# The state products of a batch gathered ahead of its four read-outs in a chunked RWKV layer

## The reference

```python
def step(s, rkvw):                       # s: state of a head, 16 x 16
    r_t, k_t, v_t, w_t = rkvw
    a = k_t[:, :, :, None] * v_t[:, :, None, :]
    out = jnp.einsum('bhk,bhkd->bhd', r_t, u * a + s)
    return (a + w_t[:, :, :, None] * s, out)
xs = tuple((jnp.moveaxis(t, 1, 0) for t in (r, k, v, w)))
_, outs = jax.lax.scan(step, s0, xs)     # 128 steps; s0 comes with the input
att = jnp.moveaxis(outs, 0, 1).reshape(b, l, E)
```

## Time and profile before

| what | us |
|---|---|
| median of 3 runs | 1643.91 (1643.78 to 1644.02) |
| the profiled execution | 1644.96 |
| its span, first to last instruction | 1643.2 |
| PE busy | 1560.6 (95%) |
| PE weight loads busy | 1156.4 (70%) |
| DVE busy | 966.8 (59%) |
| POOL busy | 604.9 (37%) |
| ACT busy | 518.5 (32%) |
| a round in the steady part (`V0` of round 7 at 763.55, of round 8 at 860.77) | 97.22 |

### The profile page before, as it was taken

One profiled execution on the slowest core, in us unless ns is written; L12 is line 12 of the kernel. 1 busy time (PEld: TensorE's weight loads), 2 busy tenths in 40 slices (PEclk: granted clock), 3 DMA queues, 4 the chain that ended last, 5 costly groups with the idle time before them and its releaser, 6 DMA issues.

```text
span 1643.2 us, 45840 instructions
## 1 busy us (share of the span) xinstructions
PE 1560.6 (95%) x19880; PEld 1156.4 (70%) x19880; DVE 966.8 (59%) x1990; ACT 518.5 (32%) x910; POOL 604.9 (37%) x512
## 2 busy tenths in 40 slices
PE   7989799999999999999999999999999999999888
PEld 7767576777777677776767677677767767777554
DVE  2555647567574755757475674746657475664542
ACT  1213323234232333323233233333323223342331
POOL 2442414426152442615335261432525244251411
PEclk9989899999999999999999999999999999999998
DMA  7010101102020110202011020200102011010200
GB/s 278 6 46 11 52 21 42 42 21 64 6 64 23 35 50 12 72 6 63 24 34 51 5 66 20 61 25 24 62 4 65 22 35 50 8 64 7 70 11 26
DMA packets 56424, 67.72 MB, mean 41 GB/s; under 512 B 23264, under 2 KB 40032, under 8 KB 55200
## 3 DMA queue, kind: packets, MB, share of 16 engines
q1 hardware_dynamic: 56224, 64.79, 12.3%
HBM read 43.75 MB, written 8.39 MB: 32 GB/s over the span
## 4 chain that ended last, share of the span: by engine, by line
PE 79%; DVE 9%; ACT 5%; POOL 5%; issue 3%; DVEq 0%; ACTq 0%; POOLq 0%
PE pair L1132 35%; PE pair L1140 17%; PE at_ps L1066 3%; PE at_ps L1059 3%; PE pair L1164 2%; POOL x L472 2%; PE kv_ps L1088 2%; DVE bonv L576 2%; PE att_ps L1123 2%; PE pair L1185 2%; ACT at L889 2%; POOL cen L498 2%; DVE x L695 1%; PE pair L1221 1%; PE pair L1148 1%
## 5 line engine op out<-in xcount | busy, mean ns | idle before, releaser
L1132 PE MATMUL pair<-x,wts 128*128 128x256 f32 x2048 | 467.0, 384 | 12.7 <-POOL x L472 12.6
L1132 PEld LDWEIGHTS pair<-x,wts 128*128 128x128 f32 x2048 | 382.6, 190 | 74.6 <-DVE x L695 14.6
L472 POOL TENSOR_TENSOR x<-x,xnT 128x1024 f32<-128x1024 f32 x80 | 173.5, 2178 | 300.8 <-DVE x L695 300.8
L695 DVE SCALAR_TENSOR_TENSOR x<-pair,vecs,sx 128x256 f32<-128x256 f32 x320 | 131.1, 476 | 199.0 <-PE pair L1164 150.2
L889 ACT ACTIVATE at<-at_ps 128x512 f32<-128x512 f32 x128 | 76.2, 595 | 204.6 <-PE at_ps L1066 202.2
L576 DVE SCALAR_TENSOR_TENSOR bonv<-rT,vecs,kT 128x128 f32<-128x128 f32 x128 | 59.1, 522 | 126.8 <-ACT rT L880 116.8
L483 POOL TENSOR_TENSOR bonv<-bonv,p 128x256 f32<-128x256 f32 x32 | 40.2, 1258 | 215.4 <-DVE p L711 215.4
L1066 PE MATMUL at_ps<-rm,kc 128*16 128x128 f32 (+1 forms) x2048 | 111.0, 276 | 0.0
L1140 PE MATMUL pair<-wts,sx 128*128 128x512 f32 x240 | 107.0, 599 | 4.1 <-ACT cen L875 4.1
L1140 PE MATMUL pair<-wts,cen 128*128 128x512 f32 x240 | 110.8, 604 | 0.0
L1140 PE MATMUL pair<-wts,yT 128*128 128x512 f32 x240 | 107.2, 599 | 0.8 <-POOL yT L510 0.8
(11 more groups left out here) (194 smaller groups left out, 2616.9 us busy)
## 6 DMA issues: line engine op xcount, KB each, us to landing
rm<-rst SPq DMA_DIRECT2D x1024, 12.0 KB, 1.8
xu<-in_x SPq DMA_DIRECT2D x16, 512.0 KB, 4.1
wts<-in_wts SPq DMA_DIRECT2D x8, 1024.0 KB, 13.8
kvs<-in_s SPq DMA_DIRECT2D x32, 256.0 KB, 2.9
s<-in_s SPq DMA_DIRECT2D x32, 256.0 KB, 2.9
x<-in_x SPq DMA_DIRECT2D x15, 512.0 KB, 4.6
out<-sx SPq DMA_DIRECT2D x15, 512.0 KB, 3.0
prev<-in_prev SPq DMA_DIRECT2D x32, 4.0 KB, 3.9
```

Source lines behind the costliest of these rows:

```text
L472: gp.tensor_tensor(t, t, xnT[:, :, :, 1:L1].rearrange("p g b t -> p (g b) t"), ALU.add).then_inc(x5_ready, 1)
L695: last = ve.scalar_tensor_tensor(seqs(x5[q], g), ps[:, :, g * L:(g + 1) * L], vecs[:, vec, g:g + 1], seqs(sx, g), ALU.add, ALU.mult)
L1132: last = pe.matmul(ps[:, g // 2, TB * (g % 2):TB * (g % 2 + 1)], wts[:, m, k, g * P:(g + 1) * P], source[:, k, :], start=(k == 0), stop=(k ...
```

## The change

The products with the states leave `read_out` and become a task of their own, `st0` or `st1`: eight products in a row (four units, two states), behind the waits that stood in `V0` or `V4`. In PE's lists `st0` stands right ahead of `V0`, `st1` right ahead of `V4`. A `V` now is its wait for `E` and its sixteen small products. The new semaphore `states_read` counts the two tasks, and the loads of `s0` and `kvs` wait for it and no longer for `read_done`. `S0` then waits for the `st1` of the round before, where it waited for that round's `V7`; `S1` and `F0` wait for `st0`, where they waited for `V3`. The lists of all other engines are unchanged, SP's too.

```diff
-PE_ORDER = [... "A0", "wv.1", "V0", "c02_1", "c1v_1", "A1", "V1", ...
-            "V4", "wo.0", ...
+PE_ORDER = [... "A0", "wv.1", "st0", "V0", "c02_1", "c1v_1", "A1", "V1", ...
+            "st1", "V4", "wo.0", ...
...
             def load_s0(blk, b):
-                if blk.past(UNITS, G * b):
-                    sp.wait_ge(read_done, blk.count(UNITS, G * b))
+                if blk.past(2, b):
+                    sp.wait_ge(states_read, blk.count(2, b))
...
             def load_first(blk, b):
-                if blk.past(UNITS, 4 * (b + 1) - UNITS):
-                    sp.wait_ge(read_done, blk.count(UNITS, 4 * (b + 1) - UNITS))
+                if blk.past(2, b - 1):
+                    sp.wait_ge(states_read, blk.count(2, b - 1))
...
+            def from_states(at_, b):
+                pe.wait_ge(kvs_ready, at_.count(2, b + 1))
+                pe.wait_ge(s0_in, at_.count(32, 16 * (b + 1)))
+                pe.wait_ge(rchain, at_.count(2 * NR, NR * (b + 1)))
+                if at_.past(2, b - 1):
+                    pe.wait_ge(attT_ready, at_.count(2, b - 1))
+                for g in range(G):
+                    pe.matmul(att_ps[:, 0, b, g, :], s0[:, g, :], rst[:, b, g, R64A:RST], start=(g == 0), stop=False,
+                              skip_group_check=True)
+                    last = pe.matmul(att_ps[:, 1, b, g, :], kvs[b][:, g * P:(g + 1) * P], rst[:, b, g, R64B:R16C],
+                                     start=(g == 0), stop=False, skip_group_check=True)
+                last.then_inc(states_read, 1)
+
             def read_out(at_, n):
                 b, g = n // G, n % G
                 o = att_ps[:, :, b, g, :]
-                if g == 0:
...
-                pe.matmul(o[:, 0, :], s0[:, g, :], rst[:, b, g, R64A:RST], start=(g == 0), stop=False,
-                          skip_group_check=True)
-                pe.matmul(o[:, 1, :], kvs[b][:, g * P:(g + 1) * P], rst[:, b, g, R64B:R16C], start=(g == 0),
-                          stop=False, skip_group_check=True)
                 pe.wait_ge(at_ready, at_.count(UNITS, n + 1))
```

More of the change, by code:

```diff
@@ L61 @@
     "kt0": 0, "kt1": 0, "kv0": 0, "kv1": 0, "F0": 1, "F1": 0, "dec0": 0, "dec1": 0, "attb1": -1, "attb0": 0, "aT1": -1, "aT0": 0}
-PE_ORDER = ["mixWV", "kt0", "V7", "kv0", "wv.0", "aT1", "A0", "wv.1", "V0", "c02_1", "c1v_1", "A1", "V1", "z", "v.0",
+PE_ORDER = ["mixWV", "kt0", "V7", "kv0", "wv.0", "aT1", "A0", "wv.1", "st0", "V0", "c02_1", "c1v_1", "A1", "V1", "z", "v.0",
             "decay", "v.1", "A2", "V2", "mixKR", "A3", "V3", "yT", "k.0", "k.1", "mixG", "kt1", "A4", "kv1", "r.0", "aT0", "r.1",
-            "V4", "wo.0", "wo.1", "A5", "g.0", "g.1", "x2T", "V5", "xT", "c02_0", "A6", "V6",
+            "st1", "V4", "wo.0", "wo.1", "A5", "g.0", "g.1", "x2T", "V5", "xT", "c02_0", "A6", "V6",
             "kk.0", "kk.1", "c1v_0", "rr.0", "rr.1", "h", "A7"]
@@ L84 @@
                 "g.1", "h", "c1v_0"],
-           LAST: ["kt0", "V7", "kv0", "wv.0", "aT1", "A0", "wv.1", "V0", "A1", "c02_1", "V1", "c1v_1", "A2", "V2",
-                  "yT", "A3", "V3", "kt1", "wo.0", "kv1", "wo.1", "aT0", "A4", "V4", "yT@0", "A5", "V5", "x2T", "A6", "V6",
+           LAST: ["kt0", "V7", "kv0", "wv.0", "aT1", "A0", "wv.1", "st0", "V0", "A1", "c02_1", "V1", "c1v_1", "A2", "V2",
+                  "yT", "A3", "V3", "kt1", "wo.0", "kv1", "wo.1", "aT0", "A4", "st1", "V4", "yT@0", "A5", "V5", "x2T", "A6", "V6",
                   "wo@0", "A7", "V7+", "kk.0", "aT1+", "kk.1", "x2T@0", "rr.0", "rr.1", "kk@0", "yT@1", "rr@0"],
@@ L236, in build @@
         wts_in = [sem(f"wts_in{m}") for m in range(8)]
-        s0_in, kvm_ready, decayed = sem("s0_in"), sem("kvm_ready"), sem("decayed")
+        s0_in, kvm_ready, decayed, states_read = sem("s0_in"), sem("kvm_ready"), sem("decayed"), sem("states_read")
         first_in = [sem(f"first_in{b}") for b in range(NB)]
@@ L1325, in step @@
                             turn_att(at_.plus(AHEAD[name]), int(name[2:]))
+                    elif name in ("st0", "st1"):
+                        if units(i):
+                            from_states(at_, int(name[2:]))
                     elif name[0] == "A":
```

## The result

The changed kernel takes 1683.71 us (1682.25 to 1684.27, 4 runs) against 1643.97 (1643.78 to 1646.98, 4 runs) for the kernel before: a ratio of 1.0236, 95% interval 1.0218 to 1.0254. It is slower, as forecast, by 39.7 us where the sum said 32.1. Its profiled execution has a span of 1682.5 us against 1643.2.

A forecast was written before the change was run, and what follows sets the result against it. PE taken as mostly the bound (1302.0 of 1336 us busy, 79% of the chain). Rounds 2 to 14 24.7, rounds 0 and 1 5.5, round 15 1.4, late loads 0.5: 32.1 us more, forecast 1676; range 1660 to 1697.

The forecast's parts named there:

- the likeliest case: The forecast of 1676 us itself, slower than the kernel before; chance 0.54, its own range 1665 to 1686.
- Price of a pair: One product with each state on PE: 0.23 us a product, 0.46 a pair; three pairs more cost 1.38 (1.02 to 1.62).
- `st0`: Three pairs more ahead of `V0`, rounds 2 to 14: 1.38 us, less 0.4 absorbed, leaves 0.98 a round.
- The absorbed part: Of the 1.38 us ahead of `V0`, 0.37, rounded to 0.4, is free because `c1v_1` waits for DVE anyway.
- `V1`, `V2`, `V3`, `V6` give nothing: These read-outs lose a pair each and gain 0: their small products wait for ACT's eviction, PE idling 0.69 us.
- `st1`: Three pairs more ahead of `V4`: 1.38 us whole on the path in rounds 0 to 14, free in round 15.
- `V5` gives nothing: Its pair stands between `g` and `xT`, which waits for the gate: 0 gained, the wait grows from 0.72 to 1.18 us.
- `V7` gives 0.46 back in rounds 2 to 14: Its pair stands between `kt0` and `kv0` with no wait around it, so 0.46 us a round is gained.
- The loads gain nothing, SyncE's queue holds `S0`: `S0` is issued 0.04 us after `M1`'s last transfer; the queue, not the semaphore, holds it, so loads start as now.
- The 0.5 us for late loads: 0.5 us in all, for rounds 2 to 14 where `S0` lands after PE, earlier by 0.46, needs it.
- Rounds 0, 1 and 15: `V0` waits for a load there, so 1.38 us for each `st0`, unabsorbed; sums 5.5 for rounds 0 and 1, 1.4 for 15.
- Rival A: From `A2` to `k` PE's clock falls, 1.69 us in each of rounds 1 to 14, 23.7 more: 1700 us; chance 0.26.

The follow-up runs named there:

- experiment 5: The kernel before, with the state pairs of `V1`, `V2`, `V3` and `V6` left out, so the result lacks them: 1644.93 us, ratio 0.9997.
- experiment 3: The kernel before, with only the pairs of `V5`, `V6`, `V7` gathered ahead of `V4` and the old waits of the loads: 1666.57 us, ratio 1.0127.
- experiment 4: The kernel before, with only the pair of `V7` moved, to `V4`: ratio 1.0036, 5.9 us.
- experiment 1: The changed kernel, with the loads of the two states waiting for the read-outs again, as before the change: 1683.31 us, ratio 1.0233.
- experiment 6: The changed kernel, with `S0` of the next block moved in SyncE's queue from behind `M1` to ahead of `M0`: 1668.62 us, ratio 1.0144.

## Why the prediction was right, and where its terms were off

The mechanism was right. Products were taken from places where ACT, a gate or a copy covered them, and put on PE's path; the loads gained nothing. The time, 1683.7, lies within the likeliest case's own range (1665 to 1686), 7.7 above the forecast of 1676 and near that range's upper end. No single term at its other bound would have reached it: the dearest variants of the sum come to 38 us, or 1682, and the range was drawn wider than they are without a working. Step by step:

- *Price of a pair*, 0.46 forecast: right. Three pairs more took 1.34 (1.82 less the 0.48 of a read-out with one pair), against 1.38; the bounds of 0.17 and 0.27 a product weren't needed.
- *`st0`*, 0.98 a round forecast: 0.77. The absorbed part was 0.57, not 0.4. Without the wait `c02_1`'s second product is followed by `c1v_1` after 0.86, not 0.95 as taken from the start of `A6`, and `c1v_1` itself runs 0.1 shorter (0.43 to the transposes, against 0.54). 0.21 a round, 2.7 us too much.
- *`V1`, `V2`, `V3`, `V6` give nothing*: right, shown by experiment 5 on its own.
- *`st1`*, 1.38: right (1.34).
- *`V5` gives nothing*: right in rounds with `xT`, whose wait grew to 1.11 (1.18 forecast); in round 14, where `xT` is missing, `c02_0` begins no earlier either (3.19 us after the first transpose of `x2T`, where it was 3.20), and a fall of the clock came behind its longer wait.
- *`V7` gives 0.46 back in rounds 2 to 14*: wrong. This is the step that failed. I wrote "no wait around it" and read that as "on the path". PE had no wait there because `V7` was just as long as ACT's copy of the turned k. It gave 0.04, so 5.5 us were missing from the sum, and experiments 3 and 4 show it.
- *The loads gain nothing, SyncE's queue holds `S0`*: right (experiments 1 and 6). The 0.5 us for late loads was 0, since PE did not come earlier after all.
- *Rounds 0, 1 and 15*, 1.38 for each `st0`: too little in round 0, where the clock was at its lower level behind the wait for the load and the products ran at half speed (3.43 instead of 1.38), too much in round 1 (0.64: a load that came 0.30 earlier and a clock that rose sooner took back most of the 2.56 of slow products), and too little in round 15 (3.84 in all from `kt0` on, 1.4 forecast). That `st1` is nearly free in round 15 was right: the tail's first transpose comes 4.92 after `V4`'s first state product instead of 4.65, and its wait grew from 1.75 to 2.54. Round 14 cost 3.67 from the `xT` before it, 1.6 of them more than a steady round. These are mis-sized terms: the sum was made at full speed. Together they are some 5 us too little, about as much as `V7`.
- *Rival A* (the clock falls ahead of `k`): it does not, in any steady round; `k` is 7.14 at 1.00. The page of the Trainium skill that spoke for it, "TensorE: Matmul & The Clock Gate", Part 4, would have made this the likelier case; the steady rounds, with `yT` and 0.79 of idle behind two gaps of 0.69, don't bear that out, though they don't show how a transpose counts.

The misses in the sum partly cancel (2.7 too much, 5.5 and some 5 too little), so that 32.1 against the spans' 39.3 looks better than its terms.

Open: why the clock falls where it does in rounds 14 and 15. In round 14 the length of the wait is not enough to tell, as the kernel of experiment 6 shows. Round 15's 3.84 is largely a sum of such falls, which no kernel varied alone: the first half of `wo` takes 5.37 us at a granted clock of 0.68 where it took 3.67 at 1.00, and a run in the tail takes 5.24 where it took 6.52, which gives 1.3 back.

## What to carry to other kernels

Before an instruction is moved, ask of its old place what would be waited for if it were gone: here six of the eight pairs of a round (`V1`, `V2`, `V3`, `V5`, `V6`, `V7`) stood in such covers, and at `V7` no wait could be seen, because the cover fitted to 0.1 us. Read the other engine's finish time there, not the idle column. A semaphore that is released earlier gives nothing while the load stands behind other transfers in its queue; moved to a place where the queue idles, it gave 15 us. And since sums commute, such products can be put after the part they wait beside, into a place where the engine idles: that version is 0.8% faster than the kernel before.

## What the runs showed of the hardware

A stream of matmuls with a 128x128 float32 stationary and 64 moving columns, its two sources in turn, ran at 0.22 to 0.23 us a product (two records): 780.89, 781.12. At the lower clock the same products started 0.43 apart (round 0, 1.82 us against 3.58 for the eight). A wait of 1.77 or 1.78 us ahead of `c02_0` went with a granted clock of 0.56 to 0.66 behind it in five of six profiles and with 1.00 in the sixth; behind 1.39 us in the same place it was always 1.00, and behind 0.69 three times within 16 us and 0.79 after them, too. Elsewhere 1.99 us of idle left the clock at 1.00, and 1.27 us was followed by 0.57. A wait that ends does not return its time in full when the next one stands behind it: in round 0 the load's 3.89 us became 3.03 us of DVE.
